# Stage 4 of a fused four-layer kernel: when absolute values, comparisons, statistics and turned tiles are issued

## The chip, the cores and the metric

The kernel is one program on one core of a Trainium2 chip. A core has five engines that run their own instruction streams and meet only at semaphores: TensorE (PE, matrix multiplication into the eight PSUM banks), VectorE (DVE), ScalarE (ACT), GpSimd (POOL), and SyncE (SP), which here only starts transfers. The metric is the device time of one execution in microseconds (us). The changed kernel has the same inputs, outputs and arithmetic.

## The reference

Input x is (2, 1024, 512) in float32, handled as 2048 rows of 512. Four residual blocks follow each other, each as `x = x + layernorm(block(layernorm(x)))`: a small attention over head groups, a feed-forward block with ternary weights, a causal attention with 16 heads, and a feed-forward block with 2:4 sparsity. Only the last is touched here:

```python
def _sparsify_2to4(h):
    g = h.reshape(B, S, I // 4, 4)
    _, idx = jax.lax.top_k(jnp.abs(g), 2)
    mask = (pos == idx[..., 0:1]) | (pos == idx[..., 1:2])
    return (g * mask.astype(g.dtype)).reshape(B, S, I)
h = jax.nn.silu(x @ w_gate) * (x @ w_up)      # (rows, 2048)
h_sparse = _sparsify_2to4(h)                  # of each four neighbours the two of largest magnitude stay
out = h_sparse @ w_down                       # (rows, 512)
```

## The kernel before

**Tiles and steps.** Stage 4 runs over four tiles of 512 rows (k = 0 to 3) and, in each, 16 slices of 128 hidden units, so 64 steps s with k = s // 16. Hidden units lie on partitions. Four consecutive steps, a group g = s // 4, hold the four members of each 2:4 quartet, one member to a step, so a comparison between members is an elementwise one between four arrays of 128 x 512. Every operand of a product is split in two parts, high and low, and each product is three matmuls.

**TensorE** (`pe_program`, lines 2049 to 2135). In step s `gate_up(s)` runs 12 matmuls for gate, called g(s) here, and 12 for up, u(s); then `down4(q)` runs 12 for each slice q in `quarters[s]`, called d(q): none in steps 0 to 7, two in step 8, then one a step with a gap at each new tile. Gate, up and the turned tiles share PSUM banks 4 to 7 in rotation (`fours`, `bank4`, lines 416 to 457), so each waits (`wait4`) until the fourth one before it was read: normally u(s) waits for hm(s-2) and g(s) for silu(s-2). At a change of tile (steps 14 and 15) two turned tiles of the next 512 rows, t(i), are put ahead of g(s), each four 128 x 128 transposes; there u(14) waits for hm(13), t(6) and t(7) for the low parts of t(4) and t(5), and u(15) for hm(14). g(16) waits for all four turned tiles.

**ScalarE** (`act_program`, lines 1543 to 1567). In step s: the silu of g(s); `split_w` for gate and up of step s+3 and down of slice s-4, which writes the high part of the weights; and `absolute(s)`, the absolute value of the product hm(s) into `ab4` (line 1488). `absolute` stands behind the three splits, except in steps with s % 4 == 3, where it stands ahead of them. In steps 13 to 15 of a tile it also normalizes the next rows (`norm4`) and writes the high part of turned tiles (`turn4`).

**GpSimd** (`pool_program`, lines 1755 to 1773). It writes the low part of the same three weights, in the same order, each when its high part is there; and it turns the variance of rows into their scale (`stats`, a power and a multiplication on 128 x 1).

**SyncE** (lines 638 to 654) loads weights in blocks of 1 MB, four steps' worth; it asks for a block when GpSimd has finished the block that lies in its place.

**VectorE** (`dve_program`, lines 1035 to 1120) runs in this order, and in no other, since an engine takes its instructions in order:

- `gate_up(s)`: hm(s) = PSUM of u(s) times silu(s), into `hm4`; the last thing of every step.
- `sparse(g - 1, 0)` in step 4g: all six comparisons of the group's four absolute values, as three instructions of 3, 2 and 1 x 512 elements (`compare`, line 1042).
- `sparse(g - 1, 1)` in step 4g+1: `count`, eight additions and subtractions in bf16, and four masks applied to `hm4`.
- `sparse(g - 1, 2)` in step 4g+2: four copies into the high part and four subtractions for the low part of the sparse rows (`HH4`, `HHx`), called HH here; d(q) waits for them.
- in step 11 of a tile the statistics of the next four row tiles, in steps 14 and 15 `turn4`, the low part of turned tiles, behind `sparse`.

Behind step 63 comes a tail for the last group: compare, count and low part in two halves of 256 columns, then the last 48 matmuls, the last statistics and rows.

Of the kernel before, what the change touches and what calls it, by code (L numbers as in the profile page):

```python
# [9 lines left out]
ALU = mybir.AluOpType  # L10
# [41 lines left out]
def network(nc, x_d, Wq_d, bq_d, Wkv_d, bkv_d, w1_d, w2_d, w3_d, qw_d, kvw_d, cw_d, wg_d, wu_d, wd_d,  # L52
# [18 lines left out]
    with ctx:  # L71
# [609 lines left out]
        def dve_program(e):  # L681
# [3 lines left out]
            def tt(out, a, b, op):  # L685
                return e.tensor_tensor(out, a, b, op)  # L686
# [352 lines left out]
                sl = slice(i * 128, (i + 1) * 128)  # L1039
                split_lo(bank4("t", t), xT4[k % 2][:, 0, :, sl], xT4[k % 2][:, 1, :, sl], 1.0, "xT4")  # L1040

            def compare(a, cm, W):
                tt(cm[:, 0:3, :], a[:, 0:1, :].broadcast_to([128, 3, W]), a[:, 1:4, :], ALU.is_ge)
                tt(cm[:, 3:5, :], a[:, 1:2, :].broadcast_to([128, 2, W]), a[:, 2:4, :], ALU.is_ge)
                return tt(cm[:, 5, :], a[:, 2, :], a[:, 3, :], ALU.is_ge)

            def count(cm, h):
                c01, c02, c03, c12, c13, c23, s0 = (cm[:, n, :] for n in range(7))
                w.wait_ge(S["dvs"], did(tt(s0, c01, c02, ALU.add)))
                tt(s0, s0, c03, ALU.add)  # L1050
                w.wait_ge(S["dvs"], did(tt(c03, c03, c13, ALU.add)))
                tt(c03, c03, c23, ALU.add)
                w.wait_ge(S["dvs"], did(tt(c13, c12, c13, ALU.add)))
                tt(c13, c13, c01, ALU.subtract)
                w.wait_ge(S["dvs"], did(tt(c23, c23, c02, ALU.subtract)))
                w.wait_ge(S["dvs"], did(tt(c23, c23, c12, ALU.subtract)))
                for n, (c, op, v) in enumerate(((s0, ALU.is_ge, 2.0), (c13, ALU.is_ge, 1.0), (c23, ALU.is_ge, 0.0),
                                                (c03, ALU.is_le, 1.0))):
                    last = stt(h[:, n, :], c, v, h[:, n, :], op, ALU.mult)
                return last  # L1060

            def sparse(g, phase):

                h = hm4[:, g % 2]
                if phase == 0:
                    w.wait_ge(S["ab"], 4 * g + 4)
                    w.wait_ge(S["ey"], 16)
                    compare(ab4, cm4, 512).then_inc(S["cma"], 1)
                if phase == 1:
                    w.wait_ge(S["cma"], g + 1)  # L1070
                    count(cm4, h).then_inc(S["hmk"], 1)
                if phase == 2:
                    w.wait_ge(S["hmk"], g + 1)
                    w.wait_ge(S["ep"], 16)
                    for r in range(4):
                        q = 4 * g + r
                        if q >= 6:
                            w.wait_ge(S["dd"], dd_at(q - 6))
                        n = did(e.tensor_copy(sparse4(q, 0), h[:, r, :]))  # L1079
                    for r in range(4):  # L1080
                        q = 4 * g + r
                        w.wait_ge(S["dvs"], n - 3 + r)
                        tt(sparse4(q, 1), h[:, r, :], sparse4(q, 0), ALU.subtract).then_inc(S["hh4"], 1)
# [18 lines left out]
            for s in range(64):  # L1102
                k, g = s // 16, s // 4
                if g >= 1 and s % 4 == 0:
                    sparse(g - 1, 0)
                if k < 3 and s % 16 == 11:
                    for i in range(4):
                        w.wait_ge(S["d_xb%d" % ((k + 1) % 2)], 16 * ((k + 1) // 2 + 1))
                        stats(96 + 4 * (k + 1) + i, xb[(k + 1) % 2][:, i, :], EPS, "mv7")
                if g >= 1 and s % 4 == 1:  # L1110
                    sparse(g - 1, 1)
                if g >= 1 and s % 4 == 2:
                    sparse(g - 1, 2)
                if k < 3 and s % 16 in (14, 15):
                    i = 4 * (k + 1) + 2 * (s % 16 - 14)
                    turn4(i)
                    turn4(i + 1)
                gate_up(s)
                if k > 0 and s % 16 == 6:
                    post4(k - 1)  # L1120


            def last_compare(part):
                cols = slice(256 * part, 256 * part + 256)
                w.wait_ge(S["dvs"], did(compare(ab4[:, :, cols], cm4[:, :, cols], 256)))

            def last_count(part):
                cols = slice(256 * part, 256 * part + 256)
# [33 lines left out]
        def act_program(e):  # L1162
# [380 lines left out]
            for s in range(64):  # L1543
# [7 lines left out]
                w.wait_ge(S["g4"], s + 1)  # L1551
                wait_row4("s", s)
                e.activation(row4("s", s), PS[:, bank4("g", s), :], ACT.Silu, scale=1.0, bias=0.0).then_inc(S["si"], 1)

                if s % 4 == 3:
                    absolute(s)
                if s > 0:
                    split_w("g", s + 3)
                split_w("u", s + 3)
                split_w("d", s - 4)  # L1560
                if s % 4 != 3:
                    absolute(s)
                if k > 0 and s % 16 == 6:
                    for i in range(4):
                        w.wait_ge(S["rs8"], 4 * (k - 1) + i + 1)
# [17 lines left out]
        def pool_program(e):  # L1583
# [3 lines left out]
            def tt(out, a, b, op):  # L1587
                return e.tensor_tensor(out, a, b, op)  # L1588
# [165 lines left out]
                    split_w("u", step // 2 - 1)  # L1754
            for s in range(64):
                k = s // 16
                if k < 3 and s % 16 == 11:
                    for i in range(4):
                        n = 4 * (k + 1) + i
                        stats(96 + n, "mv7", "rs7", n)  # L1760
                if s > 0:
# [425 lines left out]
```

## Time and profile before

| | |
|---|---|
| median of 3 runs | 1397.03 us (1394.22 to 1397.66) |
| profiled execution | 1397.03 us, of it the span 1395.3 us |
| PE (matmul) busy | 1329.8 us, 95% |
| VectorE busy | 1038.5 us, 74% |
| GpSimd busy | 694.1 us, 50% |
| ScalarE busy | 666.0 us, 48% |
| granted TensorE clock, mean | 0.996 of full |

The shares are over the whole span with its four stages; what holds in stage 4, from about 845 us to the end, has to be read from that stretch. In the rows below, `L686` and the like are lines of the kernel; many helpers share one line, so the tile's name tells what a row is: `hm<-PS,sl` is hm(s), `cm<-ab` a comparison, `cm<-cm` a count, `hm<-cm,hm` a mask, `HH<-hm` and `HHx<-hm` a high part, `HH<-hm,HH` a low part, `ws_g<-rw` a split of weights, `xT4b` a turned tile.

### The profile page before, as it was taken

Reading aid. Unit: us, or ns where it says so; the run is one execution under the profiler, and the core shown is the slowest. Engines: PE = TensorE matmul, PEld = TensorE weight load, DVE = VectorE, ACT = ScalarE, POOL = GpSimd, SP = SyncE. Lnnn points to the kernel's source line nnn. Section 1 sums busy time; section 2 is a strip of 40 time slices with the busy share of each in tenths; the row PEclk is TensorE's granted clock in tenths of the full one; section 3 lists DMA queues with packets and bytes.
Section 4 is the critical chain, followed back from the end, with each engine's and each line's share of the span. In section 5 each row is a group of like instructions: output and inputs, shape, how many; then the busy total and the mean of one; then the engine's idle time right before and its main releaser. Section 6 shows DMA issues by size and latency. Waiting matters only on the chain.

```text
span 1395.3 us, 19463 instructions
## 1 busy us (share of the span) xinstructions
PE 1329.8 (95%) x7206; PEld 912.9 (65%) x7206; DVE 1038.5 (74%) x1959; ACT 666.0 (48%) x1153; POOL 694.1 (50%) x836
## 2 busy tenths in 40 slices
PE   6989999999999899999999999998999999999997
PEld 5875446556455454555555467787888788878886
DVE  5898575665857758677666443998889878988897
ACT  6664342232325545455555575445454544454442
POOL 2576241421313413332433366776678768866863
PEclk9999999999999999999999999999999999999999
DMA  9100210204113213123013223122323422322300
GB/s 334 74 1 1 76 61 16 91 1 121 53 46 99 77 25 85 49 70 119 24 54 90 86 92 151 62 98 95 115 86 134 151 108 87 134 112 91 121 31 30
DMA packets 46270, 116.86 MB, mean 84 GB/s; under 512 B 3420, under 2 KB 4448, under 8 KB 42336
## 3 DMA queue, kind: packets, MB, share of 16 engines
q1 hardware_dynamic: 45104, 114.31, 24.0%
q8 instruction: 57, 0.93, 0.3%
q10 hardware_dynamic: 1072, 1.31, 0.3%
q14 instruction: 37, 0.30, 0.1%
HBM read 92.28 MB, written 23.07 MB: 83 GB/s over the span
## 4 chain that ended last, share of the span: by engine, by line
PE 61%; DVE 26%; ACT 5%; POOL 4%; issue 3%; DMA 1%; POOLq 0%; DVEq 0%; ACTq 0%
PE PS L1784 59%; DVE cm L686 7%; DVE SM L702 2%; DVE PS L919 2%; DVE HH L686 2%; DVE hm L695 2%; PE PS L1793 2%; DVE hm L686 1%; DMA rw<-in_L_ffn_w_up 1%; DVE HH L1079 1%; ACT EX L1349 1%; POOL SM L1588 1%; DVE HHx L1079 1%; DVE SM L698 1%; POOL ws_u L1588 1%
## 5 line engine op out<-in xcount | busy, mean ns | idle before, releaser
L1349 ACT ACTIVATE EX<-PS 128x512 f32<-128x512 f32 (+3 forms) x384 | 170.3, 494 | 134.4 <-PE PS L1784 132.6
L1588 POOL TENSOR_TENSOR SM<-SM 128x1 f32<-128x1 f32 x128 | 84.6, 661 | 214.4 <-DVE SM L692 210.6
L919 DVE CUSTOM_DVE_ANT_0 PS<-PS,MW 128x128 f32<-128x128 f32 (+3 forms) x256 | 122.5, 504 | 62.9 <-PE PS L1784 62.6
L1588 POOL TENSOR_TENSOR ws_g<-rw,ws_g 128x512 fp32r<-128x512 f32 x64 | 113.9, 1780 | 92.8 <-ACT ws_g L1166 92.8
L1784 PE MATMUL PS<-KG,QG 96*128 96x512 f32 (+3 forms) x384 | 134.8, 381 | 17.4 <-DVE SM L919 7.5
L1703 POOL TENSOR_SCALAR_AFFINE_SELECT EX<-EX 128x128 f32<-128x128 f32 x256 | 74.7, 302 | 149.0 <-ACT EX L1349 146.5
L1588 POOL TENSOR_TENSOR ws_u<-rw,ws_u 128x512 fp32r<-128x512 f32 x64 | 125.7, 1964 | 34.1 <-ACT ws_u L1166 34.1
L1784 PE MATMUL PS<-QG,KG 98*128 98x512 f32 (+3 forms) x384 | 131.3, 376 | 3.1 <-ACT EX L1349 2.7
L1784 PE MATMUL PS<-ws_d,HH 128*128 128x512 f32 x528 | 125.8, 389 | 0.9 <-DVE HH L686 0.8
L686 DVE TENSOR_TENSOR cm<-cm 128x512 bf16<-128x512 bf16 (+1 forms) x136 | 124.8, 948 | 2.4
L1784 PEld LDWEIGHTS PS<-QG,KG 98*128 98x128 f32 x384 | 69.6, 190 | 71.9 <-issue 45.6
L698 DVE TENSOR_REDUCE SM<-PS 128x1 f32<-128x512 f32 x128 | 87.7, 685 | 36.4 <-PE PS L1784 36.2
L1784 PEld LDWEIGHTS PS<-ws_d,HH 128*128 128x128 f32 x528 | 98.9, 188 | 22.2 <-issue 1.2
L1588 POOL TENSOR_TENSOR ws_d<-rw,ws_d 128x512 fp32r<-128x512 f32 x64 | 101.0, 1579 | 14.3 <-ACT ws_d L1166 14.3
L1784 PEld LDWEIGHTS PS<-KG,QG 96*128 96x128 f32 x384 | 72.2, 190 | 49.9 <-DVE SM L919 20.0
L686 DVE TENSOR_TENSOR cm<-ab 128x512 bf16<-128x512 f32 (+4 forms) x51 | 95.6, 1927 | 11.2 <-ACT ab L1491 11.2
L1784 PE MATMUL PS<-xT4a,ws_u 128*128 128x512 f32 x384 | 94.1, 395 | 4.9 <-DVE hm L686 4.8
L1491 ACT ACTIVATE ab<-hm 128x512 f32<-128x512 f32 x64 | 40.4, 632 | 120.9 <-DVE hm L686 120.9
L1784 PE MATMUL PS<-xT4b,ws_u 128*128 128x512 f32 x384 | 92.5, 390 | 0.8 <-DVE hm L686 0.7
L1784 PE MATMUL PS<-xT4a,ws_g 128*128 128x512 f32 x384 | 92.7, 390 | 0.0
L1784 PE MATMUL PS<-xT4b,ws_g 128*128 128x512 f32 x384 | 92.5, 390 | 0.0
L1166 ACT ACTIVATE ws_u<-rw 128x512 fp32r<-128x512 f32 x64 | 72.2, 1128 | 41.3 <-DMA rw<-in_L_ffn_w_up 41.3
(203 smaller groups left out, 2825.5 us busy)
## 6 DMA issues: line engine op xcount, KB each, us to landing
rw<-in_L_ffn_w_gate SPq DMA_DIRECT2D x16, 1024.0 KB, 5.1
rw<-in_L_ffn_w_up SPq DMA_DIRECT2D x16, 1024.0 KB, 7.1
rw<-in_L_ffn_w_down SPq DMA_DIRECT2D x16, 1024.0 KB, 7.9
QG<-qs SPq DMA_DIRECT2D x48, 256.0 KB, 4.2
raw<-in_L_ffn_w SPq DMA_DIRECT2D x3, 2816.0 KB, 11.6
qs<-stg SPq DMA_DIRECT2D x16, 512.0 KB, 3.5
xA<-xs SPq DMA_DIRECT2D x2, 2048.0 KB, 7.8
ys<-xA SPq DMA_DIRECT2D x4, 1024.0 KB, 4.2
```

Of the source, the lines that this page charges most:

```text
L686: return e.tensor_tensor(out, a, b, op)
L695: return e.scalar_tensor_tensor(out=out, in0=a, scalar=s, in1=b, op0=op0, op1=op1)
L698: return e.tensor_reduce(out, a, AX.X, op)
L702: w.wait_ge(S["dvs"], did(e.bn_stats(st, src)))
L919: last = e.tensor_tensor_reduce(out=p, in0=p, in1=MW[:, 512 - k1 + k0:512], scale=1.0, scalar=BIG, op0=ALU.add, op1=ALU.max, accum_out=m1)
L1079: n = did(e.tensor_copy(sparse4(q, 0), h[:, r, :]))
L1166: return e.activation(out, in_, ACT.Copy, scale=scale, bias=0.0)
L1349: e.activation(EX[:, n % 16, 0:W], PS[:, score_bank(n), 0:W], ACT.Exp, scale=ISQ, bias=0.0).then_inc(S["ex"], 1)
L1491: e.activation(ab4[:, s % 4, :], hm4[:, s // 4 % 2, s % 4, :], ACT.Abs, scale=1.0, bias=0.0).then_inc(S["ab"], 1)
L1588: return e.tensor_tensor(out, a, b, op)
L1703: e.affine_select(out=p, in_=p, compare_op=ALU.is_ge, fill=0.0, base=0, pattern=[[1, 128]], channel_multiplier=-1).then_inc(S["sel"], 1)
L1784: return e.matmul(out, l, r, start=start, stop=stop, skip_group_check=free)
```

## The change

Four things are reordered; no instruction of arithmetic is added or removed except in the tail, where the last group's first three comparisons are made in full width ahead of hm(63). ScalarE issues `absolute(s)` right behind the silu in every step. VectorE makes the three comparisons among the members 0, 1 and 2 (two instructions) ahead of hm(4g+3), in the new phase -1, and the three with member 3 (one instruction) in step 4g+4; the columns of `cm4` are renumbered accordingly. The statistics of the next rows are made two in step 11 and two in step 12, on VectorE and on GpSimd. In step 14 the two turned tiles' low parts come ahead of `sparse(g - 1, 2)`.

```diff
-            def compare(a, cm, W):
-                tt(cm[:, 0:3, :], a[:, 0:1, :].broadcast_to([128, 3, W]), a[:, 1:4, :], ALU.is_ge)
-                tt(cm[:, 3:5, :], a[:, 1:2, :].broadcast_to([128, 2, W]), a[:, 2:4, :], ALU.is_ge)
-                return tt(cm[:, 5, :], a[:, 2, :], a[:, 3, :], ALU.is_ge)
+            def compare_three(a, cm, W):
+
+                tt(cm[:, 0:2, :], a[:, 0:1, :].broadcast_to([128, 2, W]), a[:, 1:3, :], ALU.is_ge)
+                return tt(cm[:, 2, :], a[:, 1, :], a[:, 2, :], ALU.is_ge)
+
+            def compare_last(a, cm, W):
+
+                return tt(cm[:, 3:6, :], a[:, 0:3, :], a[:, 3:4, :].broadcast_to([128, 3, W]), ALU.is_ge)
...
+                if phase == -1:
+                    w.wait_ge(S["ab"], 4 * g + 3)
+                    w.wait_ge(S["ey"], 16)
+                    compare_three(ab4, cm4, 512)
                 if phase == 0:
                     w.wait_ge(S["ab"], 4 * g + 4)
-                    w.wait_ge(S["ey"], 16)
-                    compare(ab4, cm4, 512).then_inc(S["cma"], 1)
+                    compare_last(ab4, cm4, 512).then_inc(S["cma"], 1)
...
-                if k < 3 and s % 16 == 11:
-                    for i in range(4):
+                if k < 3 and s % 16 in (11, 12):
+                    for i in range(2 * (s % 16) - 22, 2 * (s % 16) - 20):
                         w.wait_ge(S["d_xb%d" % ((k + 1) % 2)], 16 * ((k + 1) // 2 + 1))
                         stats(96 + 4 * (k + 1) + i, xb[(k + 1) % 2][:, i, :], EPS, "mv7")
                 if g >= 1 and s % 4 == 1:
                     sparse(g - 1, 1)
-                if g >= 1 and s % 4 == 2:
-                    sparse(g - 1, 2)
+
                 if k < 3 and s % 16 in (14, 15):
                     i = 4 * (k + 1) + 2 * (s % 16 - 14)
                     turn4(i)
                     turn4(i + 1)
+                if g >= 1 and s % 4 == 2:
+                    sparse(g - 1, 2)
+                if s % 4 == 3:
+                    sparse(g, -1)
                 gate_up(s)
...
-                w.wait_ge(S["dvs"], did(compare(ab4[:, :, cols], cm4[:, :, cols], 256)))
+                w.wait_ge(S["dvs"], did(compare_last(ab4[:, :, cols], cm4[:, :, cols], 256)))
...
                 e.activation(row4("s", s), PS[:, bank4("g", s), :], ACT.Silu, scale=1.0, bias=0.0).then_inc(S["si"], 1)
-
-                if s % 4 == 3:
-                    absolute(s)
+                absolute(s)
                 if s > 0:
                     split_w("g", s + 3)
                 split_w("u", s + 3)
                 split_w("d", s - 4)
-                if s % 4 != 3:
-                    absolute(s)
```

GpSimd's loop takes the same two-step form of the statistics.

## Rows read from the trace of the kernel before

**Rows 1.** The page's head.
```profile
span 1395.3 us, 19463 instructions
```
**Rows 2.** Timeline of TensorE: start, length, engine, line, instruction, tiles, count, idle before.
```profile
872.21 2.88 PE L1784 MATMUL PS<-xT4a,ws_g 128*128 128x512 f32 x12
874.93 2.88 PE L1784 MATMUL PS<-xT4a,ws_u 128*128 128x512 f32 x12
...
888.41 4.49 PE L1784 MATMUL PS<-xT4a,ws_u 128*128 128x512 f32 x12 [2.44 <-DVE hm L686]
...
950.75 2.98 PE L1784 MATMUL PS<-xT4a,ws_u 128*128 128x512 f32 x12 [2.36 <-DVE hm L686]
...
1377.17 11.58 PE L1784 MATMUL PS<-ws_d,HH 128*128 128x512 f32 x48 [0.79 <-DVE HH L686]
```
**Rows 3.** Busy time in one window: PE, PEld, DVE, ACT, POOL, granted clock, DMA.
```profile
888.40:890.00 1.60, 1.59 (x4) 1.31 (x5) 1.60 (x5) 1.60 (x3) 0.00 (x0) 0.50 0.00 0
```
**Rows 4.** TensorE's waits from 842 us on: total us, times, longest.
```profile
PE PS L1784 <- DVE hm L686: 5.5, 3, 2.4
PE PS L1793 <- DVE xT4b L695: 3.7, 2, 1.9
...
PE PS L1793 <- DVE xT4a L695: 1.0, 2, 0.8
```
**Rows 5.** Timeline of VectorE around the first late blocks.
```profile
868.36 6.22 DVE L686 TENSOR_TENSOR cm<-ab 128x1536 bf16<-128x1536 f32 x3 [0.70 <-ACT ab L1491]
...
875.11 7.60 DVE L686 TENSOR_TENSOR cm<-cm 128x512 bf16<-128x512 bf16 x8
882.75 4.92 DVE L695 SCALAR_TENSOR_TENSOR hm<-cm,hm 128x512 f32<-128x512 bf16 x4
...
957.47 1.28 DVE L695 SCALAR_TENSOR_TENSOR xT4b<-PS,xT4b 128x512 fp32r<-128x512 f32 x2
958.66 0.68 DVE L686 TENSOR_TENSOR hm<-PS,sl 128x512 f32<-128x512 f32 x1
```
**Rows 6.** VectorE's groups by form, 898 to 904.3: count, busy us, mean ns, idle.
```profile
L686 DVE TENSOR_TENSOR cm<-ab 128x1024 bf16<-128x1024 f32 x1 | 2.6, 2599 | 0.0
L686 DVE TENSOR_TENSOR cm<-ab 128x512 bf16<-128x512 f32 x1 | 2.1, 2066 | 0.0
L686 DVE TENSOR_TENSOR cm<-ab 128x1536 bf16<-128x1536 f32 x1 | 1.8, 1759 | 0.7 <-ACT ab L1491 0.7
```
**Rows 7.** The same view from 1065 to 1075.
```profile
L686 DVE TENSOR_TENSOR cm<-ab 128x1024 bf16<-128x1024 f32 x1 | 1.2, 1212 | 0.0
L686 DVE TENSOR_TENSOR cm<-ab 128x512 bf16<-128x512 f32 x1 | 0.7, 679 | 0.0
```
**Rows 8.** Groups by form, 842 to 1395: GpSimd's low part of gate weights.
```profile
L1588 POOL TENSOR_TENSOR ws_g<-rw,ws_g 128x512 fp32r<-128x512 f32 x60 | 107.6, 1794 | 89.5 <-ACT ws_g L1166 89.5
```
**Rows 9.** Timeline of VectorE: high and low parts of one group, undisturbed.
```profile
1190.29 1.42 DVE L1079 CAST HH<-hm 128x512 fp32r<-128x512 f32 x4
1191.63 2.48 DVE L686 TENSOR_TENSOR HH<-hm,HH 128x512 fp32r<-128x512 f32 x4
```
**Rows 10.** Groups by form on VectorE, 1013 to 1017.3: one count.
```profile
L686 DVE TENSOR_TENSOR cm<-cm 128x512 bf16<-128x512 bf16 x1 | 0.4, 424 | 0.0
```
**Rows 11.** The chain that ended last, in order of time: start, length, what.
```profile
1080.12 7.42 DMA rw<-in_L_ffn_w_up
```
**Rows 12.** Timeline of ScalarE at the first change of tile.
```profile
948.38 1.12 ACT L1166 ACTIVATE ws_u<-rw 128x512 fp32r<-128x512 f32 x1 [2.80 <-DMA rw<-in_L_ffn_w_up]
...
950.64 0.63 ACT L1491 ACTIVATE ab<-hm 128x512 f32<-128x512 f32 x1 [0.62 <-DVE hm L686]
951.18 0.80 ACT L1169 ACTIVATE sl<-xb,SM 128x512 f32<-128x512 f32 x1
951.88 0.58 ACT L1166 ACTIVATE xT4b<-PS 128x512 fp32r<-128x512 f32 x1
```
**Rows 13.** Timeline of VectorE in the tail: the first half's three comparisons.
```profile
1363.16 2.99 DVE L686 TENSOR_TENSOR cm<-ab 128x768 bf16<-128x768 f32 x3 [0.70 <-ACT ab L1491]
```

More of the change, by code:

```diff
@@ L1040, in turn4 @@
                 split_lo(bank4("t", t), xT4[k % 2][:, 0, :, sl], xT4[k % 2][:, 1, :, sl], 1.0, "xT4")
-            def compare(a, cm, W):
-                tt(cm[:, 0:3, :], a[:, 0:1, :].broadcast_to([128, 3, W]), a[:, 1:4, :], ALU.is_ge)
-                tt(cm[:, 3:5, :], a[:, 1:2, :].broadcast_to([128, 2, W]), a[:, 2:4, :], ALU.is_ge)
-                return tt(cm[:, 5, :], a[:, 2, :], a[:, 3, :], ALU.is_ge)
+            def compare_three(a, cm, W):
[3 more added lines that the diff above has]
+                return tt(cm[:, 3:6, :], a[:, 0:3, :], a[:, 3:4, :].broadcast_to([128, 3, W]), ALU.is_ge)
             def count(cm, h):
-                c01, c02, c03, c12, c13, c23, s0 = (cm[:, n, :] for n in range(7))
+                c01, c02, c12, c03, c13, c23, s0 = (cm[:, n, :] for n in range(7))
                 w.wait_ge(S["dvs"], did(tt(s0, c01, c02, ALU.add)))
@@ L1756, in pool_program @@
                 k = s // 16
-                if k < 3 and s % 16 == 11:
-                    for i in range(4):
+                if k < 3 and s % 16 in (11, 12):
+                    for i in range(2 * (s % 16) - 22, 2 * (s % 16) - 20):
                         n = 4 * (k + 1) + i
```

## The prediction

> **What bounds the kernel now.** I read the page first: one core, span 1395.3 us [rows 1] in an execution of 1397.03 us, so 1.7 us lie around the span; the median of the three runs is the same 1397.03 us and needs no correction. The change touches stage 4 only, the last 550 us. Its TensorE timeline comes next, because in nearly every line of it twelve matmuls follow twelve others with no gap: a block shows 2.88 us and the next one starts 2.72 us after it [rows 2]. The reader is to look for the few lines that carry an idle time. I name them by the step s (0 to 63) and by the block: g(s) gate, u(s) up, d(q) down, t(i) a turned tile.
>
> - A, u(7) at 888.41: it was due at 885.8, so 2.6 us late, and its block took 4.49 instead of 2.88 us, 1.6 more [rows 2], because the granted clock was 0.50 there [rows 3].
> - B, u(14) at 950.75, 2.36 us idle [rows 2]; C, the turning t(6) soon after, 1.8 us, one of the two waits on xT4b [rows 4]. With the small gaps at their starts they make 4.6 us.
> - D and E, the same place for tiles 2 and 3. D has the two waits on xT4a, 1.0 us in all, E the second on xT4b, 1.9 [rows 4]; with the gaps at their starts I take 1.7 and 2.2 us.
> - F, one wait on hm of 0.7 us: the three on hm sum to 5.5 [rows 4], and A and B take 2.44 and 2.36 of it.
> - The tail: 0.79 us before the last 48 matmuls [rows 2] and 0.4 us inside them, since 48 blocks of 2.72/12 us should take 10.9 plus 0.2, and take 11.58.
>
> That is 4.2 + 4.6 + 1.7 + 2.2 + 0.8 + 1.3, about 15 us, the most that any reordering can give: the matmuls themselves are untouched. The waits say who ends these stalls: VectorE, by a product hm or by a turned tile's low part [rows 4]. u(s) needs the product hm(s-2) (at a tile change hm(s-1)), because it reuses that bank. So next I read VectorE's timeline before A.
>
> **VectorE before A.** After hm(3) comes the comparison of group 0, 6.22 us; then hm(4); then counts and masks, 7.60 + 4.92 us; only then hm(5), at 887.6 [rows 5]. Three comparisons of 1536, 1024 and 512 elements take 1.76, 2.60 and 2.07 us there [rows 6], but 1.21 and 0.68 us for the last two in another group [rows 7]. Each of those two lost about 1.4 us, and each such loss fell while GpSimd ran a split of a weight (1.79 us in the mean [rows 8]). I therefore price it so: one VectorE instruction with two inputs in SBUF loses 1.4 us per GpSimd split that runs beside it. A step has three splits: 4.2 us. The Trainium skill, "SBUF — State Buffer", Who interferes with whom, says it as an exclusive lock on a shared port pair: such an instruction of VectorE contends with a GpSimd one that reads SBUF, and the one issued first holds it. By that rule nothing in this change removes a collision; it only moves them, which speaks against it; the sum below has the same outcome from the rows alone.
>
> **Part 1, comparisons in two parts.** Per group the instructions and elements are the same (1024 + 512, then 1536). The first two now run ahead of hm(4g+3), in time in which VectorE often waits for TensorE; they cost 1.9 us clean, 4.6 us if both collide. Behind hm(4g+3) only 1536 elements remain: 1.8 us, at most 3.1, instead of 6.2. For group 0 this takes 3.1 to 4.5 us off the path to hm(5). Counts and masks start near 873.0, after hm(4), which waits for u(4), instead of 875.1. Their clean price is 8 x 0.39 + 4 x 0.62 = 5.6 us (0.39 a little under the 0.42 us that one count shows [rows 10], since neighbours overlap; 0.62 as for each subtraction of HH [rows 9]), plus 4.2 for three splits: 9.8 us, so hm(5) ends near 883.5. That is ahead of 885.8: A goes, the half clock with it. What is late next: ScalarE now splits behind abs(s), so the splits of step 5 run from 884.1, and HH of group 0 (3.9 us clean [rows 9] plus 1.4 x 3) ends near 891.3; hm(6) ends at 892.0, while u(8) is ready at 885.81 + 2 x 2.72 = 891.25. A stall of 0.8 us is left, u(8) starts at 892.05 and not at 895.55 (888.41 plus the slow and one plain block): **-3.5 us**. The bounds: -4.3 (no stall), and -2 if counts and masks take the 12.5 us of before and HH follows as late.
> Of TensorE's clock: [rows 3] show 0.50 after the idle of A, and no such level after B and C. The Trainium skill, "TensorE: Matmul & The Clock Gate", Part 1, says that throttled is the default and activity releases it; by that rule alone a stall of 0.8 us could again bring a slow stretch. From rows it is worth at most 1.6 us, and I keep it in the range.
>
> **Part 2, absolute values at once.** In 48 of 64 steps abs(s) moves ahead of the splits of gate, up and down (s % 4 = 3 had it there already). The abs is awaited sooner, which gives the early comparison its input. But abs(s) waits for hm(s), and behind it in ScalarE's queue now stand two splits of about 1.03 us and one of 0.5, then silu(s+1); behind these GpSimd's low parts, and behind those SyncE's requests for the next 1 MB of weights (7.42 us from request to use [rows 11]). In the steady part the splits of step s are used at g(s+3), some 19 us after u(s) ends; even an hm that is 10 us late leaves 4 us or more after 3.3 us of abs and split. Cost there: 0; the cover is that lead of three steps, and when it goes, each late g costs what it is late (0 to 1 us near g(8)). The weight block asked for in step 4g lands about 11 us after hm(4g), and hm(4g+1) follows 10.5 us after it: 0 to 1.5 us of ScalarE's wait, not on TensorE's path.
>
> **Part 3, turned tiles ahead of the sparse rows.** This is where it can be lost. Before, hm(13) ended at 950.6 (0.1 ahead of u(14)), HH ran at once, then the low parts of t(4), t(5) at 957.47, then hm(14) to 959.34 [rows 5]: 8.7 us; and t(6) waited for it, C. ScalarE had done its splits before abs(13), and was at the high part 1.24 us after abs(13) began [rows 12]. Now VectorE's t(4) waits for ScalarE's chain behind hm(13): abs 0.2 + 0.54, splits 1.02 + 1.02 and half of that for the down split, norm 0.70, high part 0.5 [rows 12], 4.5 us; t(5) is 1.2 us behind; low parts to +6.5; HH 3.9 us, since the three GpSimd splits (from +1.8, 3 x 1.7) are over by +6.9; hm(14) ends at +11.1. Queued behind the waiting t(4) are HH and hm(14), and TensorE's u(15) waits for hm(14). Without any wait u(15) starts 2.72 (u) + 2.72 (d) + 0.8 (t) + 2.72 (g) = 9.0 us after u(14). Before, it started 11.4 us after u(14): 9.0, C and two start gaps. So C's wait moves from t(6) to u(15), and shrinks from 2.4 to about 2.2 us if u(14) was itself waiting for hm(13); to nothing if hm(13) is 2 us ahead of u(14).
> For tile 1: VectorE is busy without a break from hm(3) to hm(13), so hm(13) comes earlier by about what was taken out ahead of hm(3), 3.1 to 4.5 us less new collisions: 947.2. TensorE would be ready at 950.75 - 2.6 - 3.5 = 944.6. B's stall stays, 2.6 us; u(15) at 947.2 + 11.2 = 958.4 against 962.1: still **-3.5 us**, nothing more at B and C. The bounds: u(15) later by 4.2 us (HH collides with all three splits, 8.1 us), so +0.7 in all, and earlier by 4.6 more (B and C both gone), so -8.1.
>
> **Part 4, statistics over two steps.** The same four triples of instructions, about 1.0 us each; two move behind hm(4g+3) into step 12. GpSimd's power and scale likewise, so the down split of step 11, which frees the next block of weights, comes 1 to 3 us sooner. On VectorE this is 2 us less ahead of hm(11), 2 us more ahead of hm(12): 0 for tile 1, where nothing idles. For tiles 2 and 3 VectorE has caught up: before, hm(28) waited for TensorE. There I expect hm(29) 0 to 3 us earlier relative to TensorE, so D and E give up 0 to 2 us each; I take **-0.5 and -0.6**.
>
> **F and the tail.** F sits behind group 13's comparison; 1.8 instead of 6.2 us there, though silu(56) now ends about 4.5 us after hm(55) and holds hm(56) to 2.9 us sooner: F goes, **-0.9**. In the tail each half's comparison was 2.99 us [rows 13] and becomes one instruction of 768 elements, 0.96 us (half of the 1.76 plus a start): 2.0 us sooner for the first half, 4.0 for the second, against waits of 0.79 and 0.4: **-1.3**, bounds -1.3 and 0 (the low part of the second half stands behind last_stats(0), which waits for TensorE itself).
>
> Sum: -3.5 - 0.5 - 0.6 - 0.9 - 1.3 = -6.8. 1397.03 - 6.8 = 1390.2, I say 1390.
>
> **Rivals.**
> - *VectorE's order makes it slower.* Mechanism: the wait of t(4) for ScalarE costs VectorE 4.5 us per tile change, and HH then collides with splits that GpSimd has behind. With HH at 3.9 + 3 x 1.4 = 8.1 us hm(14) ends 15.3 us after hm(13), and u(15) starts 4 us later than before relative to it: three times 4, less the 5.7 of A, F and tail, is +6.3, 1403. It decides once hm(14) ends more than about 13.4 us after hm(13) at all three changes. For it: HH of tile 1 took 957.47 - 950.5 = 7.0 us before [rows 5], so collisions are usual. Against it: the three splits should be over when HH starts. 0.12.
> - *Nothing measurable.* The first two comparisons collide in nearly every group (4.6 us), VectorE's busy chain from hm(3) to hm(13) is as long as before, and A's gain is paid back as a longer B. F and the tail remain: -2.2, 1395. For it: [rows 5] show comparison, counts and masks back to back, with no idle time to absorb a collision. 0.26.
> - *All stalls go.* hm(13), hm(29), hm(45) come ahead of need, since fewer GpSimd splits bunch beside counts: -15, 1382; with B alone, 1385. For it: counts and masks cost 5.6 us clean and took 12.5 [rows 5]. 0.16.
> - *The forecast*, own range 1387 to 1392.8: 0.46.
>
> About 0.3% (4.2 us) is what a measurement of this kernel can tell from no change. Faster by more: 0.46 + 0.16 = 0.62; within: 0.26; slower: 0.12. The range 1383 to 1399 takes in most of the large gain, all of the no-change case and the mild end of the slower one.
>
> **What would show it.** u(7) starts with no idle and no line with clock 0.50; the comparison behind hm(4g+3) is one instruction of about 1.8 us; VectorE idles about 4 us ahead of the low part of t(4), t(8), t(12), and the wait on xT4 is replaced by one on hm for u(15); the tail's 48 matmuls follow without a gap. Wrong if waits on ws_g or ws_u appear at TensorE, if u(15), u(31), u(47) each wait more than 4 us, or if A is gone and B grew by as much.

## The result, and the profile after

| | before | after |
|---|---|---|
| median | 1396.09 us (4 runs, 1394.22 to 1397.66) | 1381.43 us (4 runs, 1381.18 to 1385.79) |
| profiled execution, its span | 1397.03 us, 1395.3 us | 1381.18 us, 1379.4 us |
| PE busy | 1329.8 us, 95% | 1321.5 us, 96% |
| VectorE busy | 1038.5 us, 74% | 977.9 us, 71% |

The ratio is 0.9903 (95% interval 0.9879 to 0.9927): the kernel is 14.7 us faster, 1.0%. Forecast were 6.8 us, and the measured time lies 1.6 us under the lower end of the range. The forecast had the right sign and about half the size. The time is close to that of the rival "All stalls go" (1382), partly by luck: 2.2 us of stalls are left in stage 4, and a part of the difference lies ahead of it, as the next paragraph shows.

**Stage 4 by itself.** Spans of different executions also differ ahead of stage 4, where the code is the same, so I take a landmark that both traces have: the start of the last block of stage 3 (`PS<-CW,OT`). It stands at 842.20 before and, as this timeline of TensorE in the changed kernel shows, at 839.01 after. The lines are the landmark, the blocks that stand where A and B were, all later ones with idle time ahead of them, and the tail.

```profile
839.01 3.00 PE L1790 MATMUL PS<-CW,OT 128*128 128x512 f32 x12 [1.21 <-DVE OT L686]
...
882.65 2.88 PE L1790 MATMUL PS<-xT4a,ws_u 128*128 128x512 f32 x12
885.37 2.88 PE L1790 MATMUL PS<-xT4a,ws_g 128*128 128x512 f32 x12
888.09 2.88 PE L1790 MATMUL PS<-xT4a,ws_u 128*128 128x512 f32 x12
...
940.66 2.88 PE L1790 MATMUL PS<-xT4a,ws_u 128*128 128x512 f32 x12
...
950.23 3.00 PE L1790 MATMUL PS<-xT4a,ws_u 128*128 128x512 f32 x12 [0.31 <-DVE hm L686]
...
1083.90 3.00 PE L1790 MATMUL PS<-xT4b,ws_u 128*128 128x512 f32 x12 [0.95 <-DVE hm L686]
...
1217.59 3.00 PE L1790 MATMUL PS<-xT4a,ws_u 128*128 128x512 f32 x12 [0.95 <-DVE hm L686]
...
1361.87 11.04 PE L1790 MATMUL PS<-ws_d,HH 128*128 128x512 f32 x48
```

Against [rows 2]: A (u(7), now 882.65) and B (u(14), 940.66) have no idle time, and u(7) has its full speed, 2.88 us instead of 4.49. Three waits of u(15), u(31) and u(47) are left, 2.2 us in all; the waits on turned tiles and that of the tail are gone, as TensorE's waits of the changed kernel from 842 us on say (total us, times, longest), against four such lines in stage 4 of before ([rows 4] show three; the fourth is the 0.79 us of the tail, of [rows 2]):

```profile
PE PS L1790 <- DVE hm L686: 2.2, 3, 1.0
```

From the landmark to the end it was 1395.3 - 842.2 = 553.1 us and is 1379.4 - 839.0 = 540.4: **12.7 us less** in stage 4. The other 3.2 us of the two spans lie ahead of it. Both figures come from one profile of each kernel. Measured from the landmark, u(14) comes 6.9 us earlier than before, u(15) 8.7, u(31) 9.1, u(47) 10.3, the last 48 matmuls 12.1, the end 12.7.

**Where VectorE's time went.** Its groups by form in stage 4 (count | busy us, mean ns | idle), first before, then after, show which instructions got cheaper. The last line is GpSimd's gate split, which got dearer ([rows 8] had it at 1794 ns, idle 89.5):

```profile
L686 DVE TENSOR_TENSOR cm<-cm 128x512 bf16<-128x512 bf16 x120 | 118.7, 1019 | 2.1
L686 DVE TENSOR_TENSOR HH<-hm,HH 128x512 fp32r<-128x512 f32 x40 | 44.7, 1166 | 0.0
L1079 DVE CAST HH<-hm 128x512 fp32r<-128x512 f32 x40 | 24.6, 665 | 0.0
```
The changed kernel:
```profile
L686 DVE TENSOR_TENSOR cm<-cm 128x512 bf16<-128x512 bf16 x120 | 121.1, 1038 | 2.1
L686 DVE TENSOR_TENSOR HH<-hm,HH 128x512 fp32r<-128x512 f32 x40 | 25.3, 682 | 0.0
L1086 DVE CAST HH<-hm 128x512 fp32r<-128x512 f32 x40 | 14.6, 418 | 0.0
...
L1594 POOL TENSOR_TENSOR ws_g<-rw,ws_g 128x512 fp32r<-128x512 f32 x60 | 126.7, 2112 | 118.1 <-ACT ws_g L1176 118.1
```

The counts still lose what they lost. HH fell to its clean price: 682 ns for one subtraction and 418 for one cast (the copy into the high part), where 1166 and 665 stood. All of stage 4's comparisons, counts, masks and HH together went from 396.7 to 334.4 us, HH alone from 109.3 to 63.7. VectorE lost 62.3 us less; GpSimd's three splits together took 331.2 us before and 336.9 after, only 5.7 more. Nothing in the change touches HH in ordinary groups, so this is what the experiments had to explain. The first group shows how it looks, VectorE (above) and GpSimd (below) of the changed kernel:

```profile
865.20 1.76 DVE L686 TENSOR_TENSOR cm<-ab 128x1536 bf16<-128x1536 f32 x1 [0.70 <-ACT ab L1501]
...
869.86 6.84 DVE L686 TENSOR_TENSOR cm<-cm 128x512 bf16<-128x512 bf16 x8
876.73 2.50 DVE L695 SCALAR_TENSOR_TENSOR hm<-cm,hm 128x512 f32<-128x512 bf16 x4
879.15 0.68 DVE L686 TENSOR_TENSOR hm<-PS,sl 128x512 f32<-128x512 f32 x1
879.75 1.42 DVE L1086 CAST HH<-hm 128x512 fp32r<-128x512 f32 x4
881.09 2.49 DVE L686 TENSOR_TENSOR HH<-hm,HH 128x512 fp32r<-128x512 f32 x4
883.67 0.69 DVE L686 TENSOR_TENSOR hm<-PS,sl 128x512 f32<-128x512 f32 x1
...
926.37 0.69 DVE L686 TENSOR_TENSOR hm<-PS,sl 128x512 f32<-128x512 f32 x1 [1.77 <-PE PS L1790]
...
938.75 0.68 DVE L686 TENSOR_TENSOR hm<-PS,sl 128x512 f32<-128x512 f32 x1
943.86 0.69 DVE L695 SCALAR_TENSOR_TENSOR xT4b<-PS,xT4b 128x512 fp32r<-128x512 f32 x1 [4.43 <-ACT xT4b L1176]
...
949.40 0.68 DVE L686 TENSOR_TENSOR hm<-PS,sl 128x512 f32<-128x512 f32 x1
```
```profile
874.93 1.48 POOL L1594 TENSOR_TENSOR ws_d<-rw,ws_d 128x512 fp32r<-128x512 f32 x1
881.61 3.39 POOL L1594 TENSOR_TENSOR ws_g<-rw,ws_g 128x512 fp32r<-128x512 f32 x1 [5.20 <-ACT ws_g L1176]
884.95 1.57 POOL L1594 TENSOR_TENSOR ws_u<-rw,ws_u 128x512 fp32r<-128x512 f32 x1
```

The product hm(5) ends at 879.83. HH follows at once and is over at 883.58. GpSimd's gate split starts at 881.61, 0.52 us into the four subtractions, and takes 3.39 us instead of some 1.5: here GpSimd waits, and VectorE doesn't. Before, the same four subtractions took 5.29 us, with a split of ordinary length beside them:

```profile
889.53 5.29 DVE L686 TENSOR_TENSOR HH<-hm,HH 128x512 fp32r<-128x512 f32 x4
```
```profile
890.54 1.77 POOL L1588 TENSOR_TENSOR ws_g<-rw,ws_g 128x512 fp32r<-128x512 f32 x1 [3.43 <-ACT ws_g L1166]
892.26 1.99 POOL L1588 TENSOR_TENSOR ws_u<-rw,ws_u 128x512 fp32r<-128x512 f32 x1
```

### The profile page after: what moved, and what is told of

It reads as the page before. It is cut to its first block, busy times and chain, and to the rows that moved or that the text cites. A ratio compares the mean times of both kernels' runs of the same rounds, so it can differ in the third digit from the quotient of the medians.

```text
span 1379.4 us, 19436 instructions
## 1 busy us (share of the span) xinstructions
PE 1321.5 (96%) x7181; PEld 911.0 (66%) x7206; DVE 977.9 (71%) x1957; ACT 663.0 (48%) x1153; POOL 694.9 (50%) x836
## 4 chain that ended last, share of the span: by engine, by line
PE 77%; DVE 14%; ACT 5%; issue 2%; POOL 1%; DMA 0%; POOLq 0%; DVEq 0%; ACTq 0%
PE PS L1790 76%; DVE PS L919 2%; DVE SM L702 2%; PE PS L1799 1%; DVE cm L686 1%; DVE hm L695 1%; ACT EX L1359 1%; DVE SM L698 1%; DVE qb L692 1%; DVE SM L703 1%; ACT sl L1179 1%; ACT ws_g L1176 1%; DVE tm L686 0%; DVE qa L692 0%; DVE xT L695 0%
## 5 line engine op out<-in xcount | busy, mean ns | idle before, releaser
L1594 POOL TENSOR_TENSOR ws_g<-rw,ws_g 128x512 fp32r<-128x512 f32 x64 | 132.9, 2077 | 121.4 <-ACT ws_g L1176 121.4
L686 DVE TENSOR_TENSOR cm<-cm 128x512 bf16<-128x512 bf16 (+1 forms) x136 | 128.2, 972 | 2.4
L1594 POOL TENSOR_TENSOR ws_u<-rw,ws_u 128x512 fp32r<-128x512 f32 x64 | 111.1, 1736 | 3.1 <-ACT ws_u L1176 3.1
L686 DVE TENSOR_TENSOR cm<-ab 128x1024 bf16<-128x1024 f32 (+3 forms) x49 | 88.5, 1830 | 16.1 <-ACT ab L1501 16.1
L686 DVE TENSOR_TENSOR hm<-PS,sl 128x512 f32<-128x512 f32 x64 | 43.9, 687 | 75.1 <-ACT sl L1563 39.3
```

## The experiments

P, a theory made after the result was known: the gain is mainly one of collisions between VectorE and GpSimd, and ScalarE's order decides when GpSimd's splits fall. It has two rivals. C, in the first four experiments: the early comparisons make VectorE's chain shorter, and ScalarE's order is worth little. O, in the experiments with a memset: the absolute values come earlier, and that has a worth of its own, collisions or not. "Stage 4" is landmark to end of the profiled span: 553.1 us before, 540.4 after, one profile for each kernel. Each run was timed beside the kernel before.

**Absolute values alone.** The kernel before, and only ScalarE's order changed:

```diff
-                if s % 4 == 3:
-                    absolute(s)
+                absolute(s)
...
-                if s % 4 != 3:
-                    absolute(s)
```


> The kernel before with one edit: ScalarE issues the absolute value right behind the silu in every step; comparisons, statistics and turned tiles stay as before. The measured stage 4 became 12.7 us shorter where 6.8 were forecast; the high and low parts of group 0 cost 3.9 us and not the 8.1 I priced. Theory P (port order): since ScalarE's splits now follow hm(s), GpSimd is idle when VectorE starts behind hm(s), VectorE's chain of high and low parts runs clean (3.9 us instead of 5 to 10) and GpSimd's first split waits (3 us and more). By P this edit alone gives -5 to -9 us: the stall at u(7) stays about 2.6 us, since the comparison of 6.2 us is still ahead of hm(5), while the one at u(14) goes. Theory C (shorter chain): the gain comes from the early comparisons, and the order on ScalarE alone gives 0 to -2 us, with high and low parts as long as before.

Measured: 1383.83 us, ratio 0.9907 (0.9882 to 0.9931); stage 4 541.9 us, 11.2 less than before. One subtraction of HH takes 709 ns in the mean. This one edit gives nearly all of the change, more than either theory said; A is gone, which P had not expected. C is refuted. So is, for this edit, the idea that an earlier absolute value is what VectorE gains by: its comparisons wait for absolute values as long as before, since in the steps that they wait for (s % 4 = 3) `absolute` stood ahead of the splits already. VectorE's waits say so (total us, times, longest), the same line for both kernels:

```profile
DVE cm L686 <- ACT ab L1491: 11.2, 16, 0.7
```

Between hm(3) and hm(5) VectorE has the same instructions in the same order as before; counts and masks there take 6.83 + 2.50 us instead of 7.60 + 4.92, and that removes A. The TensorE timeline has two stalls that the full change does not have (and three of 0.2 us on turned tiles):

```profile
887.64 3.01 PE L1780 MATMUL PS<-xT4a,ws_g 128*128 128x512 f32 x12 [1.55 <-POOL ws_g L1584]
...
1369.23 5.73 PE L1780 MATMUL PS<-ws_d,HH 128*128 128x512 f32 x24 [0.65 <-DVE HH L686]
```

The first is the price of a blocked GpSimd: g(8) waits for its own split, which ran from 884.24 to 887.59, 3.35 us instead of some 1.5. In the changed kernel the same split ends at 885.00 and g(8) starts at 885.37, a margin of 0.37 us.

**All but the absolute values.** The changed kernel with ScalarE's old order, the diff above reversed.

> The changed kernel with ScalarE's order put back (absolute value behind the three splits, except in steps with s % 4 == 3). P: high and low parts are disturbed again (6 to 9 us a group) and 4 to 8 us of the gain are lost: 1386 to 1390. C: at most 2 us are lost, 1382 to 1384.

Measured: 1389.25 us, 0.9939 (0.9915 to 0.9963); stage 4 546.7, 6.3 more than the changed kernel, as P said. One subtraction of HH is back at 1053 ns, and five waits on hm sum to 6.5 us. The longest again has a slow block behind it, which is 1.7 of the 6.3 us:

```profile
957.29 4.58 PE L1794 MATMUL PS<-xT4a,ws_u 128*128 128x512 f32 x12 [2.57 <-DVE hm L686]
```

**Comparisons alone.** The kernel before with the comparisons in two parts.

```diff
+                if phase == -1:
...
+                    compare_three(ab4, cm4, 512)
                 if phase == 0:
...
-                    compare(ab4, cm4, 512).then_inc(S["cma"], 1)
+                    compare_last(ab4, cm4, 512).then_inc(S["cma"], 1)
```


> The kernel before with one edit: three comparisons ahead of hm(4g+3), three behind it, the tail included. P: the chain before u(7) is shorter by 3 to 4.5 us, so the stall at u(7) goes and with it the stretch at half clock, F and the tail's waits go too, but the stall at u(14) and the waits on xT4 stay: -4 to -6 us. C: -9 us or more, nearly the whole gain.

Measured: 1389.65 us (11 runs), 0.9954 (0.9937 to 0.9971); stage 4 546.3, 6.8 less than before. That is between what P (4 to 6) and C (9 or more) said: VectorE's own order has a worth too, where collisions exist. One subtraction of HH takes 877 ns in the mean. By itself this part is worth what I had forecast for the whole change, though it keeps 3.7 us of waits on turned tiles and has a slow block behind one of them: after 1.98 us idle and eight transposes, twelve matmuls took 4.59 us (952.22).

**All but the comparisons.** The changed kernel with the one block of comparisons, the diff above reversed.

> The changed kernel with all six comparisons together again behind hm(4g+3), the tail's too. P: the stall at u(7) is back at 1 to 3 us, the tail's waits of 1.2 us are back, the rest of the gain stays: +3 to +6 us on the changed kernel, 1384 to 1388. C: nearly all of the gain is lost, 1391 or more.

Measured: 1383.96 us, 0.9909 (0.9887 to 0.9931); stage 4 543.0, 2.6 more than the changed kernel. P had said 3 to 6 with A back at 1 to 3 us; A did not come back. Instead there is the 1.55 us wait for the split of g(8), as with the absolute values alone, and 0.7 us in the tail: with the other edits in place, the comparisons in two parts cover only these and 0.3 us elsewhere.

**No subtraction on GpSimd, old order.** The kernel before, with a memset in place of GpSimd's subtraction.

```diff
-                tt(lo, src, hi, ALU.subtract).then_inc(S["w" + kind], 1)
+                e.memset(ws[:, s % slots, 1, :].bitcast(F32), 0.0).then_inc(S["w" + kind], 1)
```


> The kernel before, in its old order, but GpSimd writes the low part of each weight as zeros with a memset (same waits, same signals, no reading of SBUF): the low parts of the weights are left out of the arithmetic. It takes the collision away by itself, without any new order. Theory P (a VectorE instruction with two SBUF inputs and a GpSimd subtraction that reads SBUF block each other): comparisons of 1024 and 512 elements fall to 1.2 and 0.7 us, counts to 0.4, high and low parts to 3.9 us a group, and stage 4 (from the last block of the projection to the end) falls from 553 to 539 to 542 us, as in the changed kernel, with the old order untouched. Rival O (order): it is the position of the absolute value in ScalarE's queue, an earlier input for VectorE, that matters, and not the port; then VectorE's pieces stay as long and stage 4 stays above 548 us.

Measured: 1379.21 us, 0.9881 (0.9847 to 0.9915). TensorE has no wait at all in stage 4. (The landmark's record is missing here, so I count from g(0), some 2.8 us later: 534.4 us, against 550.3 before and 537.6 after; expected were 539 to 542 from the landmark, some 536 to 539 from g(0).) The groups by form show the counts, 1019 ns before, and the memsets:

```profile
L686 DVE TENSOR_TENSOR cm<-cm 128x512 bf16<-128x512 bf16 x120 | 46.9, 421 | 2.0
...
L1748 POOL MEMSET ws_g<- 128x512 f32 x60 | 31.6, 527 | 300.4 <-ACT ws_g L1166 300.4
```

Comparisons, counts, masks and HH now sum to 219.9 us instead of 396.7. So before, 177 us of VectorE's stage 4 were lost to the splits, most of them in time that TensorE did not wait for; what came through to TensorE was 15.9 us. O had said that stage 4 would stay above 548 us from the landmark; it is about 537, so with the old order and the old absolute values no stall is left. The memset is also a third as long as the subtraction, so this run alone doesn't separate "reads nothing" from "shorter"; that one count takes 421 ns in the mean over 120, clean by [rows 10], speaks for the first, since some memsets do run beside counts (the eight counts from 870.97, with memsets at 870.92 and 871.44, took 3.26 us in all).

**Turned tiles behind the sparse rows again.** The changed kernel with that part undone.

```diff
+                if g >= 1 and s % 4 == 2:
+                    sparse(g - 1, 2)
                 if k < 3 and s % 16 in (14, 15):
                     i = 4 * (k + 1) + 2 * (s % 16 - 14)
...
-                if g >= 1 and s % 4 == 2:
-                    sparse(g - 1, 2)
```


> The changed kernel with the turned tiles' low parts behind the sparse rows again in step 14. In the changed kernel VectorE idles 4.4 us ahead of t(4) and u(15), u(31), u(47) wait 0.3, 0.95 and 0.95 us. P with clean high and low parts (3.9 us): VectorE would do them inside ScalarE's 4.5 us, so t(4) comes at +4.6 to +5.3 us behind hm(13) in either order and hm(14) 4 us sooner; t(6) is needed at +5.4 and waits at most 0.3 us. So -1 to -2 us of stage 4 against the changed kernel (540.4): this part of the change costs a little. Rival: the turned tile ahead is what saves 1 to 2 us at each of the three changes of tile: +3 to +6 us.

Measured: 1388.5 us (9 runs), 0.9932 (0.9911 to 0.9953); stage 4 545.8, 5.4 more. P was wrong here by its sign: this part is needed. TensorE waits for turned tiles three times, 1.5, 2.3 and 2.2 us, and behind the last of them runs slowly (eight transposes 1.69 us instead of 1.23, twelve matmuls 4.17 instead of 2.9), which is 1.7 of the 5.4 us. The cause is in VectorE's and GpSimd's timelines at the first change of tile:

```profile
941.06 0.68 DVE L686 TENSOR_TENSOR hm<-PS,sl 128x512 f32<-128x512 f32 x1
...
943.00 2.65 DVE L686 TENSOR_TENSOR HH<-hm,HH 128x512 fp32r<-128x512 f32 x2
945.58 3.75 DVE L686 TENSOR_TENSOR HHx<-hm,HHx 128x512 fp32r<-128x512 f32 x2
949.25 1.27 DVE L695 SCALAR_TENSOR_TENSOR xT4b<-PS,xT4b 128x512 fp32r<-128x512 f32 x2
```
```profile
943.53 1.58 POOL L1594 TENSOR_TENSOR ws_g<-rw,ws_g 128x512 fp32r<-128x512 f32 x1 [2.94 <-ACT ws_g L1176]
945.07 2.01 POOL L1594 TENSOR_TENSOR ws_u<-rw,ws_u 128x512 fp32r<-128x512 f32 x1
```

The split comes 0.53 us into the subtractions, as at 881.61 above, but here VectorE loses: four subtractions take 6.4 us instead of 2.5. With the turned tiles first, HH starts when the three splits are over (945.65 against 945.50), and its four subtractions take 2.5 us.

**ScalarE's turned tiles ahead of its splits.** The changed kernel; the splits of step 13 come behind step 14's turned tiles, so that VectorE's t(4) need not wait for them.

```diff
+                if k < 3 and s % 16 == 14:
+                    splits(s - 1)
...
+                if not (k < 3 and s % 16 == 13):
+                    splits(s)
```


> The changed kernel with ScalarE's three splits of step 13 moved behind the normalization and the high parts of step 14's turned tiles. It takes 2.6 us out of the chain hm(13), abs, splits, norm, high part, so VectorE's idle time ahead of t(4) falls from 4.4 to 1.9 us. P: GpSimd's splits now start at about +4.4 us, when VectorE is at its high and low parts; once VectorE streams, it is GpSimd that waits, so these stay near 4 us, hm(14) comes 2 us sooner, and the three waits of u(15), u(31), u(47) go: -2 us of stage 4, 538.4. If instead each split costs VectorE 1.4 us, as I priced it, these parts take 6 to 8 us and nothing is gained.

Measured: 1386.75 us, 0.9929 (0.9901 to 0.9957); stage 4 546.0, 5.6 more, 1.7 of it a slow block (4.56 us) behind the last of the waits. Wrong again: HH collides once more, as the other half of the expectation had it, and the loss is larger than the "nothing is gained" written there. VectorE's idle time ahead of t(4) fell from 4.43 to 1.89 us, which is what the edit is for, and HH paid for it:

```profile
941.26 0.69 DVE L695 SCALAR_TENSOR_TENSOR xT4b<-PS,xT4b 128x512 fp32r<-128x512 f32 x1 [1.89 <-ACT xT4b L1176]
...
943.72 3.49 DVE L1086 CAST HHx<-hm 128x512 fp32r<-128x512 f32 x2
947.14 2.38 DVE L686 TENSOR_TENSOR HH<-hm,HH 128x512 fp32r<-128x512 f32 x2
```

From 943.06 to 950.64 HH took 7.6 us instead of 3.8. Two of the casts, with one input in SBUF each, took 3.49 us instead of 0.76. The 4.4 us that VectorE idles in the changed kernel are the time in which GpSimd gets its splits done.

**All but the statistics.** The changed kernel with the four statistics in step 11 again, on VectorE and GpSimd.

```diff
-                if k < 3 and s % 16 in (11, 12):
-                    for i in range(2 * (s % 16) - 22, 2 * (s % 16) - 20):
+                if k < 3 and s % 16 == 11:
+                    for i in range(4):
```


> The changed kernel with the four statistics in one step again (VectorE and GpSimd). VectorE idles before hm(11) and hm(12) in the changed kernel's first tile by 0.2 and 1.8 us, so 2 us more ahead of hm(11) delay the comparison, hm(12) and hm(13) by 0 to 2 us; u(14) has about 1.3 us of margin at hm(13). Both theories: 0 to +2 us, no more; a loss of over 3 us would mean that GpSimd's bunched statistics hold the weights' splits.

Measured: 1384.88 us, 0.9912 (0.9886 to 0.9939); stage 4 542.4, 2.0 more. As expected, at its upper end.

**The product ahead of the sparse rows.** What is left are the waits for hm(14), hm(30) and hm(46), behind HH. At the changes of tile this kernel puts HH behind them.

```diff
-                if g >= 1 and s % 4 == 2:
+                if g >= 1 and s % 4 == 2 and not (k < 3 and s % 16 == 14):
                     sparse(g - 1, 2)
...
                 gate_up(s)
+                if k < 3 and s % 16 == 14:
+                    sparse(g - 1, 2)
```


> The changed kernel with one more move: in step 14 of a tile VectorE makes hm(14) ahead of the high and low parts of group 2, which then follow it. Theory P: hm(14) comes at +7 us behind hm(13) instead of +11, so u(15), u(31), u(47) no longer wait (0.31 + 0.95 + 0.95 us and the gaps at their starts, 2.7 us in all); the high and low parts run from +7 us, when GpSimd's three splits of step 13 are over, and end at +11 to +13, while d(8) needs them at +11.7: at most 1 us is given back each time. Stage 4: 538 to 540 us against 540.4. If the splits of step 14, released sooner by abs(14), collide with them in full (8 us), d waits 3 us at each change and stage 4 grows to 545.

Measured: 1379.48 us (1379.21 to 1379.81), 0.9872 (0.9858 to 0.9887); stage 4 539.0, 1.4 less. The best version, and as expected. HH now collides (2.67 + 3.74 us for its subtractions in tile 1), but little waits for it: two waits of 0.5 and 0.4 us are left in stage 4.

**The changed kernel once more**, unaltered, in the same group of runs.

> The changed kernel once more, unaltered, on the same chip and in the same rounds as its variants. Both theories: 1381 to 1384, stage 4 of 540 to 541 us; what differs between its runs is ahead of stage 4 (the start of the projection's last block between 838 and 842 us, with the granted clock of a hundred-us stretch at 0.97 to 1.00).

Measured: 1380.98 us, 0.9888 (0.9872 to 0.9905); stage 4 540.5. So a tenth of a microsecond separates two profiles of one kernel in stage 4; for the kernel before there is one profile, so its spread there isn't known. Against this run the best version gains 1.5 us in the medians; the intervals of the two ratios to before overlap, but the four times of each don't (1380.88 to 1383.17 here).

**No subtraction on GpSimd, new order.** The changed kernel with the memset.

> The changed kernel with GpSimd's memset in place of its subtraction, as in the run on the kernel before: the low parts of the weights are left out of the arithmetic. Theory P says that the new order is worth what it saves in collisions, so without them it is worth nothing: stage 4 at 537 to 539 us, within 1 us of the 537.5 that the old order gave without collisions. Rival O (the earlier inputs have a worth of their own): 2 us or more below it, 535.5 or less.

Measured: 1377.63 us, 0.9866 (0.9844 to 0.9888); from g(0) to the end 534.4 us, the same to 0.1 us as with the old order. Without GpSimd's subtractions the whole change is worth nothing in stage 4, as P said, and it does no harm there either. As a test against O this run is weak, though: with the memset the old order left TensorE no wait in stage 4, so no order could have gained anything. Against O speak the old order without any stall in the other run with a memset, and the unchanged waits for absolute values in the first experiment. That VectorE's order has a worth where collisions exist is what the comparisons alone show. Shown is also that every wait of stage 4 goes with the subtractions: of the 15.9 us that they cost TensorE before, 3.2 are left after, and 1.8 in the best version.

## Why the prediction was half right

- **The failed step is the price of HH in Part 1,** "HH of group 0 (3.9 us clean plus 1.4 x 3)", and with it Part 2's "Cost there: 0", which looked for what ScalarE's new order could cost and at nothing that it could bring. I had written the clue down myself (ScalarE "now splits behind abs(s), so the splits of step 5 run from 884.1"), and still charged HH three collisions, 8.1 us. It took 3.8 us (879.75 to 883.58), with none. With splits behind abs(s), GpSimd's come after hm(s), and HH comes right behind hm(s) too. GpSimd is idle (5.20 us in the row) when HH starts and does not get in before it ends. hm(5) ended where forecast (883.5, less the 3.2 us ahead of stage 4, is 880.3; measured 879.8). hm(6) ended at 884.4, not 888.8: its 0.8 us stall at u(8) did not come, and u(8) is 4.3 us earlier than before from the landmark (888.09 now, 895.56 before) instead of 3.5.
- **"B's stall stays" followed from it,** and from "VectorE is busy without a break from hm(3) to hm(13)". HH of group 1 took 3.8 us (9.7 before), and by hm(12) VectorE had caught up and waited 1.77 us for TensorE. hm(13) was forecast for 947.2, 944.0 after the same 3.2, and ended at 939.4: 4.6 us sooner, B's 2.6 and 2 more. Tile 1 gave 8.7 us instead of 3.5; these 5.2 are nearly all of the miss of 5.9 in stage 4. The bound of -8.1 for tile 1 was in the text, and the rival "All stalls go" stood at 0.16. (Part 3's own numbers, 958.4 against 962.1, give -3.7 and not -3.5.)
- **Part 1's own mechanism was right.** The comparison behind hm(3) is one instruction of 1.76 us, counts and masks took 9.4 us (forecast 9.8), A went, and the half clock of [rows 3] with it.
- **The price of a collision was right** and "nothing in this change removes a collision; it only moves them" was a wrong basis for the sum. One blocked instruction loses 1.4 us (2066 against 679 ns for the 512-element comparison in [rows 6, 7]; 2.65 us for two subtractions of HH at 943.00 against 1.28 undisturbed). But VectorE's losses are not a fixed sum: where GpSimd waits instead, VectorE loses nothing. GpSimd's gate split grows from 1.79 to 2.11 us in the mean, its up split falls from 1.98 to 1.74, and GpSimd, which idled 138 us in front of its splits before, idles 138 us there still. So most of the loss was not handed over, it went away. It is not always free for GpSimd to wait: with the absolute values alone it cost g(8) 1.55 us, and Part 2's "Cost there: 0" held in the change by 0.37 us.
- **Part 3's chain was right nearly to the digit.** t(4) waited 4.43 us (forecast 4.5); hm(14) ended 10.65 us after hm(13) (11.1); the wait moved from t(6) to u(15). It is 0.31 us, not 2.2, since hm(13) was 1.2 us ahead of its need; the forecast named that case. Part 3 gave the move no worth of its own, but undoing it costs 5.4 us once the absolute values come at once. The slower rival's mechanism (HH colliding at the change of tile) is real. It came in the three experiments that put HH beside the splits, and not in the change.
- **Tiles 2 and 3** gave 0.4 and 1.2 us (0.5 and 0.6 forecast); **F and the tail** 0.8 and 1.5 (0.9 and 1.3 forecast); the tail's comparison was 0.96 us, as forecast.
- **3.2 us** of the spans' 15.9 lie where the change touches nothing. (This 15.9, 1395.3 - 1379.4, only happens to equal the 15.9 us of the run with a memset.) Windows of the two traces (PE, PEld, DVE, ACT, POOL busy; granted clock, DMA) show the same 100 us of stage 3, before and after:

```profile
500.00:600.00 100.00, 95.05 (x623) 52.90 (x622) 71.12 (x209) 47.56 (x108) 27.84 (x67) 0.97 0.21 55
```
```profile
500.00:600.00 100.00, 95.13 (x637) 54.12 (x637) 70.97 (x209) 47.72 (x111) 29.84 (x71) 1.00 0.21 54
```

Over the runs the landmark stands at 838.6 to 839.0 where no window ahead of it is under 1.00, and at 839.6 to 842.2 where one or two windows of 100 us are at 0.97 or 0.98, though all these kernels have the same code there. What sets the clock in a given execution is open.

**The parts don't add.** Stage 4, us. Each alone, against before: absolute values -11.2, comparisons -6.8. Each undone in the whole: +6.3, +2.6, turned tiles +5.4, statistics +2.0. The slow blocks (1.6 us of A before, 1.7 us in each of the kernels without the absolute values and without the turned tiles) are in these figures, and one profile each doesn't show how regularly they come. The stalls are shared: A goes with either of the first two, and at a change of tile every edit moves the same product relative to the same splits.

## What to carry to other kernels

When the order on one engine changes, list what it moves on every engine downstream, and price the instructions that collide with those of a busy engine from both sides: who waits if the other is first. A short chain right behind a handoff (here hm, then HH) is cheap if the competitor's work is released behind that handoff. One experiment that takes the contention away gives the ceiling (here 15.9 us). It cannot tell whether a reorder has another worth, if it leaves no wait to remove; for that, look in the traces with the contention in place whether the inputs in question were waited for at all.

## What the runs showed of the hardware

- One VectorE instruction with two inputs in SBUF that meets a GpSimd subtraction loses 1.4 us; beside a GpSimd memset it loses nothing (421 ns for a count, against 1019 in the mean with the subtractions). The Trainium skill, "SBUF — State Buffer", Who interferes with whom, says that such an instruction contends with a GpSimd one that reads SBUF and not with one that only writes it; both runs with a memset agree. Casts with one SBUF input lost too: 3.49 us for two instead of 0.76.
- Who waits isn't settled by these start times. A split that started 0.5 us into the subtractions took 3.4 us and let them run (881.61), and one that started 0.53 us into them took 1.58 us and held them up (943.53). GpSimd had been idle 5.20 us ahead of the first and 2.94 ahead of the second. The six traces of before, of the changed kernel, and of the kernels with the absolute values alone, with the turned tiles behind, with ScalarE's turned tiles ahead and with the product ahead have 68 gate splits that started 0.50 to 0.56 us into a stretch of HH's subtractions. In 58 of them GpSimd had been idle 4.75 us or more and waited (3.35 to 3.40 us); in 10 it had been idle 1.71 to 2.94 us and VectorE waited. But at 943.51, with ScalarE's turned tiles ahead, the split came into the casts after 5.90 us idle, and VectorE lost. So the idle time goes with the outcome for the subtractions; whether it decides was not tried. The same section says that issue order decides who blocks; by the start times VectorE was first in both, so either they are not the order of issue, or something else decides as well.
- A slow block of twelve matmuls, 4.49 to 4.59 us, followed idle times of TensorE of 2.44, 2.57 and 2.37 us, and, behind eight transposes, one of 1.98 us; one of 4.17 us followed 2.23. None followed 2.36 [rows 2], 2.42 and 2.25 us. In each of the slow ones the granted clock was 0.50 for a part of the time. From these rows the idle time alone does not tell.
